# The last expert layer of a four-stage Trainium2 kernel: ranks from the upper triangle of token pairs, with the other half as column sums on TensorE

## What is computed

```python
x = x + cross_attention_0(layernorm(x), ctx, mask)
x = x + mixture_of_32_experts_0(layernorm(x))
x = x + cross_attention_1(ctx, layernorm(x), mask)
x = x + _L1_ffn_ref(_layernorm(x), router_w, W1, b1, W2, b2)      # the stage of this case

def _route(tokens, router_w):          # T = 2048 tokens of 128, E = 8 experts
    capacity = int(math.ceil(T / E * 1.25))                       # 320
    probs = jax.nn.softmax(tokens @ router_w.T, axis=-1)
    top1_idx, top1_prob = jnp.argmax(probs, -1), jnp.max(probs, -1)
    order = jnp.lexsort((-top1_prob, top1_idx))
    ...                                # rank of a token among those of its expert
    return jnp.where(rank < capacity, top1_idx, 0)

for e in range(E):                     # F = 512 hidden
    y = relu(tokens @ W1[e] + b1[e]) @ W2[e] + b2[e]
    out = out + jnp.where((final_e == e)[:, None], y, 0.0)
```

## Time and profile before

| | us |
|---|---|
| median of 3 executions | 1219.65 (1218.85 to 1220.3) |
| the profiled execution | 1218.04 |
| its span, first to last instruction | 1216.2 |
| expert layer 1 begins | about 1048.6 |
| first product of the compares | 1094.1 |
| last scatter issued | 1160.5 |
| mean granted clock of PE | 0.919 |

### The profile page before, as it was taken

The page is one execution under the profiler, slowest core; times in us unless marked ns, Lnnn a source line. Parts: engine busy times, 40 slices in busy tenths (PEclk is TensorE's granted clock), DMA queues, the critical chain, the costliest instruction groups (busy, mean ns, idle before and its releaser), DMA issues. The chain is left out here.

```text
span 1216.2 us, 25879 instructions
## 1 busy us (share of the span) xinstructions
PE 945.2 (78%) x9389; PEld 609.2 (50%) x9394; DVE 916.2 (75%) x2050; ACT 787.1 (65%) x1500; POOL 569.5 (47%) x504
## 2 busy tenths in 40 slices
PE   2688888656999954788988888888888888448656
PEld 1355555423444422355656666566656566324345
DVE  7689899656666678688887878888887877379921
ACT  2276776767555554699898989988898978232022
POOL 4100000031778841576565777766566773120425
PEclk9899999856999977799999999999999999659879
DMA  7310110040000001111111111111111110410140
GB/s 259 67 15 15 23 19 0 3 147 7 20 26 19 13 1 27 19 25 21 23 24 28 28 28 23 24 19 28 19 28 27 28 29 2 189 50 1 46 133 27
DMA packets 76175, 46.52 MB, mean 38 GB/s; under 512 B 55096, under 2 KB 72999, under 8 KB 75246
## 3 DMA queue, kind: packets, MB, share of 16 engines
q1 hardware_dynamic: 74632, 42.32, 14.6%
q0 software_dynamic: 1440, 2.82, 0.6%
HBM read 26.44 MB, written 8.77 MB: 29 GB/s over the span
## 5 line engine op out<-in xcount | busy, mean ns | idle before, releaser
L1523 POOL TENSOR_TENSOR e_p_lo<-e_probs,e_p_hi 128x1024 f16<-128x1024 f32 x64 | 136.4, 2131 | 127.5 <-ACT e_probs L1816 127.5
L1882 DVE TENSOR_REDUCE e_neg_max<-e_row_scores 128x1 f32<-128x512 f32 x256 | 169.6, 683 | 7.8 <-PE e_row_scores L1595 6.3
L1814 ACT ACTIVATE e_p_hi<-e_scores 128x512 f16<-128x512 f32 x256 | 153.3, 599 | 34.2 <-PE e_scores L1699 32.5
L1698 PE MATMUL e_scores<-e_q_stack,e_k_stack 128*128 128x256 f16 x512 | 124.2, 273 | 7.1 <-DVE e_p_lo L1887 6.8
L1506 POOL TENSOR_TENSOR e_raw<-e_raw,e_inv 128x512 f32<-128x512 f32 x90 | 92.8, 1045 | 73.2 <-DVE e_inv L1854 73.2
L1699 PE MATMUL e_scores<-e_q_high,e_k_high 128*128 128x256 f16 x512 | 124.0, 273 | 0.0
L1611 PE MATMUL e_mix<-e_v_cols,e_p_hi 128*128 128x65 f16 x1024 | 107.1, 192 | 4.4 <-POOL e_p_lo L1523 3.3
L1612 PE MATMUL e_mix<-e_v_cols,e_p_hi 128*128 128x64 f16 x1024 | 107.3, 195 | 0.0
L1613 PE MATMUL e_mix<-e_v_cols,e_p_lo 128*128 128x65 f16 x1024 | 106.7, 191 | 0.0
L1518 POOL TENSOR_TENSOR e_natural<-e_raw,e_natural 128x512 f16<-128x512 f32 x90 | 102.5, 1160 | 8.6 <-ACT e_natural L1745 8.6
L773 POOL TENSOR_TENSOR c_h_lo<-c_hidden,c_h_hi 128x512 f16<-128x512 f32 x68 | 78.7, 1157 | 57.0 <-ACT c_h_hi L978 55.8
(11 more groups left out here) (377 smaller groups left out, 2872.7 us busy)
## 6 DMA issues: line engine op xcount, KB each, us to landing
e_k_high<-e_k_stack SPq DMA_DIRECT2D x64, 128.0 KB, 2.7
e_q_high<-e_q_stack SPq DMA_DIRECT2D x32, 128.0 KB, 2.6
w<-in_w SPq DMA_DIRECT2D x2, 2048.0 KB, 9.9
c_w<-in_w SPq DMA_DIRECT2D x17, 192.0 KB, 2.4
placed_scratch<-in_no_rows SPq DMA_DIRECT2D x1, 2313.0 KB, 16.4
a_mask_q<-in_mask_q SPq DMA_DIRECT2D x4, 512.0 KB, 7.9
a_mask_k<-in_mask_k SPq DMA_DIRECT2D x1, 2048.0 KB, 13.6
parts_scratch<-a_parts SPq DMA_DIRECT2D x8, 256.0 KB, 3.3
```

Source lines behind the costliest of these rows:

```text
L1523: nc.gpsimd.tensor_tensor(p_lo[buf][i][:], probs[i][:], p_hi[buf][i][:], ALU.subtract).then_inc(lo_done[i], 1)
L1698: pe.matmul(out, k_stack[hf][:, h, cols], q_stack[hf][:, h, :], start=(kt % 2 == 0), stop=False, skip_group_check=True)
L1814: act.activation(p_hi[p % 2][i][:, at, :], scores[n % SBANKS][:], ACT.Exp).then_inc(exp_done, 1)
L1882: dve.tensor_reduce(neg_max[buf][:, 2 * i + qt:2 * i + qt + 1], row_scores[qt % RBANKS][:], AX.X, ALU.max, negate=True).then_inc(max_done, 1)
```

## The change

- The block of its own for the weights goes; SP issues the four loads in the layer's block, behind the four small ones and before the fill.
- ACT no longer waits for `w1` before the roots: it takes them first, with epsilon as a bias (a tile that POOL fills), and DVE's four additions of epsilon go. The cast of expert 0's `w1` follows the last `take`, and behind it stands a one-element `Exp`, ahead of which its function table is loaded.
- DVE's four memsets go. POOL does small ones at the start, and the tables `keys_t` and `onehot_t` have 24 rows instead of 32, all of which are written.
- The three copies of `onehot` become one instruction, PE turns `onehot` while DVE still makes the parts of `key`, into four banks (`rk` and `yb`), and ACT takes the second half of each table.
- POOL waits with the low half of the other experts' `w1` until both tables are out of PSUM.
- Seventeen small products with a matrix of ones (L2215 to L2218) give each token the number of tokens of its expert in all tiles before its own (`before`, read as `earlier`).
- Compares run over the upper triangle only: tile `t` against tiles `t` to 15, three at a time (`RT`), 51 compares with 136 tiles in all, all with `is_gt`. PE sums each result over its partitions by a product with one column of ones for each tile right of the diagonal (`lose`, 120 products of one column, the result as the stationary operand), into `lost`. The rank is count + ties + `earlier` - `lost`.
- The results of compares lie in three buffers instead of two, `lost` is copied out at three points (`lost_rows`), and PE goes on only after that.
- Places run in groups of 7, 5 and 4 tiles, in ten chained instructions as before.
- Of the 28 pieces, 20 stay in the loop of the compares and the last 8 (y pieces) come after it.

```diff
-PLACED_AT = [(0, 12), (12, 16)]
+RT = 3
+PLACED_AT = [(0, 7), (7, 12), (12, 16)]
...
-        compares = [(t, c) for t in range(NT) for c in range(T // RC)]
+        compares = [(t, c, min(c + RT, NT)) for t in range(NT) for c in range(t, NT, RT)]
...
+            sp.dma_start(w1[:], io["w1"]).then_inc(keep["w1_in"], 16)
+            sp.dma_start(b1[:], io["b1"]).then_inc(keep["b1_in"], 16)
+            sp.dma_start(w2[:], io["w2"]).then_inc(keep["w2_in"], 16)
+            sp.dma_start(b2[:], io["b2"].partition_broadcast(P)).then_inc(keep["b2_in"], 16)
             sp.dma_start(io["placed"], io["no_rows"]).then_inc(empty_out, 16)
...
+            pool.wait_ge(parts_taken, 4)
             pool.wait_ge(w_hi_done, 2)
             nc.gpsimd.tensor_tensor(w1_lo[:, 1:E1], w1[:, 1:E1], w1_hi[:, 1:E1], ALU.subtract).then_inc(w_lo_done, 1)
...
+            def lose(n):
+                t, first, end = compares[n]
+                if n - 1 in needs:
+                    pe.wait_ge(lost_read, needs.index(n - 1) + 1)
+                for c in range(max(first, t + 1), end):
+                    mm = pe.matmul(lost[:, c:c + 1], compared[:, n % 3, P * (c - first):P * (c - first) + P], ones[:, 0:1],
+                                   start=False, stop=(t == NT - 2), skip_group_check=True)
+                mm.then_inc(summed, 1)
...
-                pe.matmul(rk[n % 2][:], onehot_t[:, P * t:P * t + P], keys_t[:, RC * c:RC * c + RC], start=True, stop=True).then_inc(rank_ready, 1)
-                if n % 2 and left:
+                pe.matmul(rk[n % 2][:, 0:P * (end - first)], onehot_t[:, P * t:P * t + P], keys_t[:, P * first:P * end],
+                          start=True, stop=True, skip_group_check=True).then_inc(rank_ready, 1)
+                if n >= 2:
+                    lose(n - 2)
+                if n % 2 and len(left) > 8:
                     run(left.pop(0))
+            pe.wait_ge(rank_taken, len(compares) - 1)
+            lose(len(compares) - 2)
             while left:
                 run(left.pop(0))
...
-            act.wait_ge(keep["w1_in"], 16)
-            act.copy(w1_hi[:, 0], w1[:, 0]).then_inc(w_hi_done, 1)
...
-                act.activation(var[:, tiles], var[:, tiles], ACT.Sqrt).then_inc(root_done, 1)
+                act.activation(var[:, tiles], moments[:, tiles, 1], ACT.Sqrt, bias=eps[:]).then_inc(root_done, 1)
...
+            act.wait_ge(keep["w1_in"], 16)
+            act.copy(w1_hi[:, 0], w1[:, 0]).then_inc(w_hi_done, 1)
+            act.activation(eps[:], eps[:], ACT.Exp)
...
-            for n, (t, c) in enumerate(compares):
+            for n, (t, first, end) in enumerate(compares):
                 dve.wait_ge(rank_ready, n + 1)
...
-                for cells, op, at in ops:
-                    ins = dve.tensor_scalar(compared[:, n % 2, cells], bank[:, cells], mine, None, op, ALU.add, accum_out=counts[:, t, at:at + 1])
...
+                if n >= 3:
+                    dve.wait_ge(summed, n - 1)
+                ins = dve.tensor_scalar(compared[:, n % 3, 0:P * (end - first)], bank[:, 0:P * (end - first)], mine, None,
+                                        ALU.is_gt, ALU.add, accum_out=counts[:, t, (first - t) // RT:(first - t) // RT + 1])
...
+                for i, m in enumerate(needs):
+                    if n == min(m + 2, len(compares) - 1):
+                        at = slice(*PLACED_AT[i])
+                        dve.wait_ge(summed, m + 2)
+                        dve.tensor_copy(lost_rows[:, at], lost[:, at]).then_inc(lost_read, 1)
```

More of the change, by code:

```diff
@@ L63, in bc, with statistics @@
     return ap.unsqueeze(axis).to_broadcast(shape)
-def statistics(dve, chain, src, stats, moments, tiles):
+def statistics(dve, chain, src, stats, moments, tiles, done=None):
     for t in tiles:
@@ L72, in statistics @@
         ins = dve.bn_aggr(moments[:, t, :], stats[:, t, :])
-    chain.then(ins)
+    if done is None:
+        chain.then(ins)
+    else:
+        ins.then_inc(done, 1)
 def normed(dve, out, src, moments, inv, tiles):
@@ L2050, in experts_layer1 @@
         yb = [psum(f"yb{i}", [P, 512]) for i in range(2)]
-        rk = [psum(f"rk{i}", [P, RC]) for i in range(2)]
+        rk = [psum(f"rk{i}", [P, 512]) for i in range(2)]
+        before, lost = yb[1][:, 0:NT * E1], yb[1][:, NT * E1:NT * E1 + NT]
         small_in, empty_out = sem("small_in"), sem("empty_out")
@@ L2072, in experts_layer1, with dense_bank, dense_answers @@
         pieces += [("y", NCHUNK - 1, i) for i in range(4)]
-        compares = [(t, c) for t in range(NT) for c in range(T // RC)]
+        def dense_bank(n):
+            return hid[n if n < FB else (n - FB) % 3]
+        def dense_answers(c):
+            return yb[c == NCHUNK - 1]
+        compares = [(t, c, min(c + RT, NT)) for t in range(NT) for c in range(t, NT, RT)]
+        per_row = [len(range(t, NT, RT)) for t in range(NT)]
+        needs = [sum(per_row[:end - 1]) - 1 for _, end in PLACED_AT]
         tiles = [(0, P), (P, P), (2 * P, CAP - 2 * P)]
@@ L2178, in _ @@
                     mm.then_inc(parts_turned, 1)
+            pe.wait_ge(cleared, 4)
             pe.wait_ge(parts_taken, 4)
-            pe.wait_ge(cleared, 1)
-            left = pieces[FB:]
-            for n, (t, c) in enumerate(compares):
+            pe.matmul(before[:, 0:E1], ones[:], zeros[:], start=True, stop=False, skip_group_check=True)
+            pe.matmul(lost[:, 0:1], ones[:], zeros[:, 0:1], start=False, stop=False, skip_group_check=True)
+            for t in range(NT - 1):
+                mm = pe.matmul(before[:, E1 * (t + 1):NT * E1].rearrange("p (t e) -> p t e", e=E1), ones[:],
+                               parts[:, t:t + 1, 0, 0:E1].to_broadcast((P, NT - 1 - t, E1)),
+                               start=False, stop=False, skip_group_check=True)
@@ L2301, in centre @@
             def centre(g):
-                tiles = slice(4 * g, 4 * g + 4)
-                statistics(dve, chain, xr, stats, moments, tiles_of(g))
-                dve.tensor_scalar(var[:, tiles], moments[:, tiles, 1], EPS, None, ALU.add).then_inc(var_done, 1)
+                statistics(dve, chain, xr, stats, moments, tiles_of(g), var_done)
             def norm(g):
@@ L2332, in _ @@
             low(3)
-            chain.then(dve.memset(keys_t[:].bitcast(F32), 0.0))
-            chain.then(dve.memset(onehot_t[:].bitcast(F32), 0.0))
-            chain.then(dve.memset(counts[:], 0.0))
-            dve.memset(parts[:], 0.0).then_inc(cleared, 1)
             total, prob, rank, kept, named, away = (x[:] for x in line)
@@ L2380, in places @@
                 at = slice(first, end)
-                dve.wait_ge(rank_taken, T // RC * end)
+                dve.wait_ge(rank_taken, sum(per_row[:end]))
+                dve.wait_ge(lost_read, PLACED_AT.index((first, end)) + 1)
                 chain.then(dve.tensor_reduce(rank[:, at], counts[:, at], AX.X, ALU.add))
                 chain.then(dve.tensor_tensor(rank[:, at], rank[:, at], away[:, at], ALU.add))
+                chain.then(dve.tensor_tensor(rank[:, at], rank[:, at], earlier[:, at], ALU.add))
@@ L2385, in places @@
+                chain.then(dve.tensor_tensor(rank[:, at], rank[:, at], lost_rows[:, at], ALU.subtract))
                 chain.then(dve.tensor_scalar(kept[:, at], rank[:, at], float(CAP), None, ALU.is_lt))
[L2386 to L2389 removed]
@@ L2390, in places @@
-                chain.then(dve.tensor_tensor(named[:, at], named[:, at], rank[:, at], ALU.add))
-                chain.then(dve.tensor_scalar(away[:, at], kept[:, at], -OUTSIDE, None, ALU.mult))
-                chain.then(dve.tensor_tensor(named[:, at], named[:, at], away[:, at], ALU.add))
-                dve.tensor_copy(place[:, at], named[:, at]).then_inc(place_done, 1)
+                chain.then(dve.scalar_tensor_tensor(kept[:, at], expert[:, at], 0.0, kept[:, at], ALU.is_gt, ALU.mult))
+                chain.then(dve.scalar_tensor_tensor(named[:, at], expert[:, at], float(CAP), rank[:, at], ALU.mult, ALU.add))
```

110 lines of the change are left out of this document (53 added, 57 removed).

## The result

The changed kernel takes 1199.83 us in the median of four executions (1188.65, 1190.11, 1209.55, 1210.33), against 1219.31 before, a ratio of 0.984. Its executions fall on two values, near 1189 and near 1210, and none is near the median; over the two shorter ones alone the ratio is 0.9756, 95% interval [0.9736, 0.9775]. This second value is the changed kernel's own, as the rows show, and it is TensorE's clock in the compare loop. Both are read here.

The account below looks back on a forecast made before the run. DVE was taken to bound the compare loop. Savings of 15.8 us up to the first score product and 14.7 after it, less 0.2, made -30.3: 1187.7 for the profiled execution, 1189.3 as median, range 1182 to 1200.

Parts of the forecast that it names:

- The forecast's own case: Whole kernel: the change works as described and takes 1189 us; given an 80% chance.
- the first rival: Compare loop: TensorE's clock stays at 1.2 GHz because of short products and waits, +15 us, 1204; chance 7%.
- First score product: Layer's front, from its first load to the first score product: at 1078.3 instead of 1094.1, 15.8 us saved.
- the stall of the subtraction: Front: DVE's 7.00 us subtraction of key no longer runs beside POOL's long one, 6.7 us saved.
- What I called late next: Front: ACT, with w1's cast, two table loads, copies and the exponential, is done at 1066.7; DVE resumes 8.9 us earlier.
- Loop up to the second places: From first score product to second places: 30.4 us of DVE work plus 6.7 of waits and low clock, 37.1.
- DVE's waits in y pairs: Compare loop: DVE waits 0.42 us for PE in each of eight y pairs, 0.17 in each of twelve h pairs.
- One-column products: Column sums in the loop: 0.03 us each; a rival without overlap, up to 0.5 each, gives 1233, chance 3%.
- The 1194: Column sums in the loop: their full loading time, 0.11 us per product, some 5 us beyond DVE's slack.
- POOL's subtraction in the loop: Rival: POOL's long subtraction, moved into the loop, holds DVE's compares for its 7 us, 1196; chance 7%.
- Scatters and their meeting with the residual addition: Layer's end: nine scatters at 1.28 us follow the second places; the addition beside the last adds 1.0.
- Tail: From the last scatter's end to the end of the span: 54.7 us, unchanged.

Follow-up runs that it names:

- rows128: Changed kernel with both score-product tables at 128 rows, 104 of them zero, instead of 24: median 1189.89 us, ratio 0.974.
- r128_w1: rows128 with ACT again waiting for w1 and casting it ahead of the roots: 1201.84 us, ratio 0.982.
- r128_pool: rows128 with POOL's long subtraction no longer waiting for the tables and ACT's long w1 cast ahead of its table copies: ratio 0.98, 6.5 us over rows128.
- the 1187.42 execution: The changed kernel run once more without an edit; the profiled execution, with the clock up at the loop's start: 1187.42 us.
- nolose: Changed kernel with 50 instead of 120 one-column products and no token kept, so scatters write nothing: median 1207.32 us.
- before24: Kernel before the change, with only its two tables cut from 128 to 24 rows: median 1247.9 us against 1221.29, ratio 1.0221.
- rows64: rows128 with tables of 64 rows instead of 128, 40 of them zero: 1195.22 to 1199.7 us, ratio 0.9782.
- early_h: Changed kernel with three h pieces moved from the loop to before the transposes: 1207.49 to 1212.55 us.

## Why the prediction was right, and where it was not

The forecast was 1189 with a range of 1182 to 1200; the median of 1199.83 lies just inside. That is luck: no execution is near it, and with one more long one it would have been outside. The forecast's own case came true in half of the executions (1188.65, 1190.11), and the first rival in the other half.

- **First score product (forecast 29.7 after the layer's start).** 28.9 in the profile, 27.3 where the clock was up, 28.8 in rows128. Its two large terms hold: the table load moved from 8.5 to 1.4 us after the layer's first load, 7.1 where I had 7.2, and r128_w1 shows that such a delay counts nearly in full (7.8 of 8.9); the stall of the subtraction is worth 6.5 (r128_pool), where I had 6.7. What I called late next, ACT with its two table loads and the copies, is what DVE waits for at 1068.11.
- **The clock in the loop: the step that failed.** I gave the lower clock 7%, because of short products and waits, and held against it 1.00 in the earlier trace rows with PE as dense. Density was indeed not the trouble (PE busy 10.00 of 10 at 0.50). I had not asked what else about the products the change altered: their rows. The change has it in one line (which the diff ahead of the prediction leaves out), and I costed that at nothing. The rival was too small as well: it said +15 in the loop, where the slower profile is 20.3 over the forecast (73.0 less 52.7) and 17.2 over the faster one. It should have had some 50%, and the faster case a note that it hangs on the clock surviving a gap.
- **Loop up to the second places (forecast 37.1).** 39.5 in rows128 (1118.58 less 1079.13), 41.9 in the faster execution of the changed kernel, which lost its clock at the places. The term that the 24 rows broke is the score product at 0.16: to the next product it is 0.17 with 128 rows (1086.99 to 1087.16 in rows128), but 0.26 with 24 (1081.41 to 1081.67 below), and from three column sums to the next score product it is 0.16 instead of 0.07. A pair with a y piece and six column sums took PE 1.46 in rows128 (1086.99 to 1088.45) and 1.84 in the 1187.42 execution (1080.99 to 1082.83). So DVE's waits in y pairs, which I had at 0.42, are larger there, three times 0.66 and more in the first four; those in h pairs, which I had at 0.17, are 0.16 to 0.51. One of them in the 1187.42 execution:

```profile
1086.82 0.62 DVE L2461 TENSOR_SCALAR_CACHE_REDUCE f_compared<-f_rk,f_line 128x384 bf16<-128x384 f32 x1 [0.76 <-PE f_rk L2239]
```

  In rows128 they are near what I had, 0.57, 0.44 and 0.37 in the first four y pairs (one pair waited for nothing). What is missing there stands elsewhere: 0.8 instead of 0.2 from the first score product to the first compare, and the last compares ahead of the second places, where no piece stands between the products and I had no wait (0.55, then 0.71 at 1116.05, then 0.96):

```profile
1087.36 0.62 DVE L2465 TENSOR_SCALAR_CACHE_REDUCE f_compared<-f_rk,f_line 128x384 bf16<-128x384 f32 x1 [0.57 <-PE f_rk L2241]
...
1114.71 0.62 DVE L2465 TENSOR_SCALAR_CACHE_REDUCE f_compared<-f_rk,f_line 128x384 bf16<-128x384 f32 x1 [0.55 <-PE f_rk L2241]
...
1117.91 0.48 DVE L2465 TENSOR_SCALAR_CACHE_REDUCE f_compared<-f_rk,f_line 128x256 bf16<-128x256 f32 x1 [0.96 <-PE f_rk L2241]
```

  Why DVE waits so long in these last ones was not settled.
- **One-column products (0.03 each, or 1233 if they do not overlap).** 0.03 apart is right. Timeline of PE in the 1187.42 execution: three of them start at 1081.67, the y piece at 1081.76.

```profile
1081.41 0.33 PE L2239 MATMUL f_rk<-f_keys_t,f_onehot_t 24*128 24x384 bf16 x1
1081.67 0.23 PE L2231 MATMUL f_yb<-f_ones,f_compared 128*128 128x1 bf16 x3
1081.76 0.36 PE L2193 MATMUL f_yb<-w,f_hidden 128*128 128x128 f32 x1
```

  The Trainium skill ("TensorE: Matmul & The Clock Gate", "LDWEIGHTS (loading the stationary operand)") gives 107 ns for such a load. The group of the 120 loads agrees in duration (99 ns in that profile). Within a group of three they hide; the first of each group does not, behind a score product of 24 rows. The 1194 worked out from adding all of them did not come. What such a product costs in all is bounded by nolose: 2 to 3 us for 70 of them, nearly all at the lower clock.
- **POOL's subtraction in the loop (rival of 7%).** Did not hold the compares: beside POOL's 6.96 us (1081.37) those of three tiles are still 0.54 apart. They have one operand in SBUF.
- **Scatters and their meeting with the residual addition.** 1.28 each, as forecast. The meeting (1.0 in the sum) did not happen: the addition waits for the last y rows and began at 1131.64, after the last scatter (1128.78), since loop and y pieces ended later than I had them. In before24 it met a scatter again, and that took 2.98. The Trainium skill ("SBUF — State Buffer", "Who interferes with whom") infers that a `tensor_tensor` does not hold back descriptor generation; with 2.99 in the earlier trace rows and 2.98 here, against 0.97 for their neighbours, two traces speak against it for two operands in SBUF.
- **Tail (54.7, "unchanged").** 56.2 and 56.8 in the two profiles of the changed kernel, 56.9 in rows128, and up to 60.4 (rows64). It is 56.7 in before24 too, which has the old order of the layer, so the new order is not what lengthens it. DVE's waits in it are for PE and for earlier output scatters to land; why the tail is 2 us longer than before was not settled.

Summed for rows128, the change as I had imagined it: -16.7, -13.9 and +2.2 make -28.4, where the forecast had -30.3.

## What to carry to other kernels

When a change makes a matmul's contraction (the rows over which it sums) smaller, because the rest was only padding, the instruction is no faster, the loads next to it may come out from under it, and TensorE may lose its clock: here 24 rows in place of 128 cost 26.6 us in a kernel of 1221. In the changed kernel zeros in the other 104 rows, two memsets on an idle engine, made every execution as short as its shorter ones. Of every product that an edit touches ask all of its dimensions, and read the granted clock of the stretch before and after, not only busy shares. And where executions of one kernel fall on two values, a median says little: take a profile of each.

## What the runs showed of the hardware

- TensorE's granted clock went with the rows of the score products, and not with PE's busy time. At 24 rows it stayed at 1.2 GHz with PE busy 10.00 of 10 (40 us in a row above, and again in before24; in nolose it rose once for 3 to 4 us); at 128 rows, with the same products and order, it rose to 2.4 GHz some 4 us after the loop's start and fell in 1116 to 1118; at 64 rows it rose some 7 us after the loop's start and fell at 1112.
- At 24 rows a clock that is already at 1.00 can be held: 31 us in the 1187.42 execution (1072.96 to 1104). In early_h it fell right at the loop's start instead. What decides between these two stays open.
- Behind a product of 24 or 64 rows the load of a 128-row stationary operand did not begin until 0.26 us after the product's start (384 columns, clock 1.00), where behind one of 128 rows it began 0.01 after it, and a pair of score products with six column sums and a y piece took PE 1.84 us (24 rows) instead of 1.46.
- A DVE subtraction of 128 elements that meets a POOL subtraction, both with two operands in SBUF, takes POOL's 6.96 us plus 0.04, wherever the pair was put (before, before24, r128_pool).
- A one-column product with a new stationary operand every time starts 0.03 us after the last, within a group of three.
